# A four-layer graph attention network on one core: transposed blocks of the load stage in two PSUM banks, two segments a round

## The reference

```python
def layer(x, adj, W, a, slope):
    Wh = x @ W
    e = (Wh @ a[:64, 0])[:, None] + (Wh @ a[64:, 0])[None, :]
    e = jnp.where(e > 0, e, slope * e)
    attention = softmax(jnp.where(adj > 0, e, NEG), axis=1)
    return elu(attention @ Wh)
x = layernorm(x + layer(x, adj, W0, a0, 0.2))     # and three more
```

## Time and profile before

| | |
|---|---|
| runs | 601.85 us median (600.64 to 601.86) |
| span of the profiled execution | 859.9 us; the page gives no other time of it |
| granted clock of TensorE, mean | 0.815 |
| PE busy | 419.1 us (49%) |
| DVE busy | 349.6 us (41%) |
| ACT busy | 400.8 us (47%) |
| POOL busy | 278.0 us (32%), 292 gathers of 951 ns |
| ACT masks (L839) | 31 of 3.70 us, the last at 277.3 us |

### The profile page before, as it was taken

One profiled execution on the slowest core, in us unless ns is written; L12 is line 12 of the kernel. 1 busy time (PEld: TensorE's weight loads), 2 busy tenths in 40 slices (PEclk: granted clock), 3 DMA queues, 4 the chain that ended last, 5 costly groups with the idle time before them and its releaser, 6 DMA issues.

```text
span 859.9 us, 10681 instructions
## 1 busy us (share of the span) xinstructions
PE 419.1 (49%) x3453; PEld 334.5 (39%) x3453; DVE 349.6 (41%) x1601; ACT 400.8 (47%) x876; POOL 278.0 (32%) x296
## 2 busy tenths in 40 slices
PE   2354512246655786411129983310499633104985
PEld 1243301245543675300119862210397522004964
DVE  3035813744379598200003872300048622000587
ACT  2677612555476476200325971231269612313684
POOL 0000173140320410777710034777100437771000
PEclk9999999999999998555559995755599857555997
DMA  8999962482673100222200012222000112220000
GB/s 312 428 330 428 422 198 58 173 290 100 212 282 124 17 26 27 32 27 27 27 8 2 20 30 29 28 27 27 9 1 20 34 26 27 28 28 6 8 19 28
DMA packets 20546, 84.86 MB, mean 99 GB/s; under 512 B 6083, under 2 KB 11462, under 8 KB 16262
## 3 DMA queue, kind: packets, MB, share of 16 engines
q1 hardware_dynamic: 10102, 73.15, 21.8%
q0 software_dynamic: 9344, 9.89, 9.4%
q10 hardware_dynamic: 1040, 1.08, 0.4%
HBM read 78.72 MB, written 5.37 MB: 98 GB/s over the span
## 4 chain that ended last, share of the span: by engine, by line
another core or an unknown queue 23%; PE 17%; DVE 12%; ACT 11%; issue 9%; DVEq 0%; ACTq 0%
PE bank L709 7%; ACT arena L865 4%; PE bank L689 3%; PE bank L672 3%; ACT arena L851 2%; DVE x L1313 2%; PE bank L670 1%; DVE stats L1295 1%; PE bank L705 1%; ACT arena L875 1%; DVE arena L1232 1%; ACT arena L839 1%; PE bank L574 1%; DVE res L1292 1%
## 5 line engine op out<-in xcount | busy, mean ns | idle before, releaser
L528 POOL DMA_INDIRECT xg<-table,index x292 | 277.8, 951 | 499.4 <-DMA table<-wh 299.8
L1232 DVE CUSTOM_DVE_ANT_0 arena<-bank,arena 128x256 f32<-128x256 f32 (+3 forms) x123 | 63.4, 523 | 284.7 <-ACT arena L851 224.5
L851 ACT ACTIVATE arena<-bank,sloped_own 128x256 f32<-128x256 f32 (+3 forms) x123 | 68.5, 557 | 176.3 <-remote 109.7
L689 PE MATMUL bank<-packed,arena 128*128 128x128 f32 x339 | 68.3, 323 | 120.0 <-issue 74.0
L839 ACT ACTIVATE arena<-arena,half 128x4096 bf16<-128x4096 int32 x31 | 114.7, 3703 | 19.1 <-DMA arena<-in_adj_t 18.5
L689 PEld LDWEIGHTS bank<-packed,arena 128*128 128x128 f32 x339 | 46.0, 165 | 132.7 <-issue 118.5
L875 ACT COPY arena<-bank 128x256 f32<-128x256 f32 (+3 forms) x123 | 54.1, 446 | 75.4 <-remote 55.4
L670 PE MATMUL bank<-off_row,wall 128*128 128x256 bf16 (+3 forms) x132 | 43.9, 332 | 81.2 <-issue 58.4
L709 PE MATMUL bank<-xg,arena 128*128 128x64 f32 x486 | 73.0, 284 | 10.6 <-ACT arena L875 8.6
L709 PEld LDWEIGHTS bank<-xg,arena 128*128 128x128 f32 x486 | 63.7, 197 | 24.0 <-ACT arena L875 13.5
L1029 DVE MAX8 top<-bank 128x8 f32<-128x256 f32 x31 | 13.4, 431 | 131.5 <-remote 69.5
(11 more groups left out here) (148 smaller groups left out, 780.1 us busy)
## 6 DMA issues: line engine op xcount, KB each, us to landing
arena<-in_adj_t SPq DMA_DIRECT2D x31, 2048.0 KB
xg<-table,index POOLq DMA_INDIRECT x292
table<-wh SPq DMA_DIRECT2D x24, 132.0 KB, 1.7
arena<-in_adj SPq DMA_DIRECT2D x1, 2048.0 KB, 12.9
table<-wh ACTq DMA_DIRECT2D x1, 1056.0 KB
x<-in_x SPq DMA_DIRECT2D x1, 1024.0 KB, 15.0
out_x<-x SPq DMA_DIRECT2D x8, 128.0 KB, 1.9
packed<-in_c_packed SPq DMA_DIRECT2D x1, 312.0 KB
```

Source lines behind the costliest of these rows:

```text
L528: pool.indirect_dma_start(out=xg[:, c, :], out_offset=None, in_=table[l][0:rows, :], in_offset=bass.IndirectOffsetOnAxis(ap=index[:, c:c + ...
L689: t = nc.tensor.transpose(turned_ps[turned_bank(n)][:, c * P:(c + 1) * P], scores(l, n)[:, c * P:(c + 1) * P], ident[:, :])
L851: nc.scalar.activation(scores(l, n)[:, 0:m * P], score_ps[n % len(score_ps)][:, 0:m * P], ACT.Relu, bias=sloped_own[:, k:k + 1], scale=ALP ...
L1232: nc.vector.tensor_tensor_reduce(out=y, in0=score_ps[n % len(score_ps)][:, 0:m * P], in1=y, scale=-1.0, scalar=-FLOOR, op0=ALU.add, op1=AL ...
```

## The change

`KNOWN_MAX` goes from 3 to 2. Segments below `LATE` alternate between bank 5 and bank 7. Bank 7 is free between the last use by the load stage's projections and the first projection for layer 1, and two waits guard these ends: segment 1, the first in bank 7, waits until DVE has read the sum of layer 0 out of it, and layer 1's first projection waits until the last segment of the load stage in bank 7 (segment 19) has been copied.

```diff
-KNOWN_MAX = 3
+KNOWN_MAX = 2
...
 def turned_bank(n):
-    return n % 2 if n >= LATE else 0
+    return 0 if n % 2 == 0 else 1 if n >= LATE else 2
...
+LOAD_TURNED = max(n for n in range(LATE) if turned_bank(n) == 2) + 1
...
-        turned_ps = [banks[5], banks[0]]
+        turned_ps = [banks[5], banks[0], banks[7]]
...
                 pe.wait_ge(xt_copied, n + 1)
+                if n == GROUPS:
+                    pe.wait_ge(turned_copied, LOAD_TURNED)
...
                     pe.wait_ge(xt_copied, GROUPS)
+                if n == 1:
+                    pe.wait_ge(sum_copied, 1)
```

## The result

The changed kernel takes **576.68 us** (median of 4 runs, 575.02 to 578.31) against 601.25 us for the kernel before on the same chip (4 runs, 600.33 to 601.86): ratio 0.9599, 95% interval 0.957 to 0.9627. It is faster by 24.6 us, where 21.6 were forecast.

What follows compares the result with a forecast made beforehand. Bound: a chain of waits, PE and ACT taking turns over one bank. Terms -21.2 (turns), -1.4 (ahead of mask 19), +1.0 (behind mask 23) sum to -21.6 us: 601.85 to 580 us, forecast range 576 to 584 (0.61).

Steps and rivals of the forecast that it cites:

- The span: Whole profile: 859.9 us against 601.85 us timed; timed runs lack its standstills, so savings carry over in microseconds.
- The turns: Load stage, masks 19 to 23: PE and ACT alternate over one bank; 49.26 us becomes 27.15, counted as -21.2.
- a late PE: Masks 19 to 23: about 0.9 us of the old 49.26 is PE issuing late, left out of the saving.
- The round with the lists: PE's third two-segment round, pack of mask 21, also does list matmuls: 7.78 us instead of 7.15.
- Ahead of mask 19: ACT before mask 19 has two fewer exponentials, 2 x 0.71 us: -1.4 us.
- Behind mask 23: Group 5's combine moves behind DVE's list step of batch 5: +1 us taken, bounds 0 and +5.3.
- the 0 that I chose between 0 and 2: Masks 28 to 30, segments of tiles 1 and 2: possible further gain of 0 to 2 us, taken as 0.
- Half comes back: Rival: DVE's 5.3 us list step exposed at beats 20 and 24 loses 10.6 us again: 591 us; chance 0.15.
- No change: Rival: timed load stage is paced by something the profile distorts, such as gathers: 601.85 us; chance 0.13.
- slower: Rival: turns off the timed path, combine behind the list step at beat 25 costs up to 5.3: 607 us; chance 0.06.
- More: Rival: all 23.7 us of ACT's waits for PE go, plus 1.4 and 2 us: 575 us; chance 0.05.

Runs made afterwards that it cites:

- the second profile: The kernel before, unchanged, timed and profiled once more: 601.44 us, ratio 0.9998.
- b: The changed kernel with KNOWN_MAX back at 3, so two banks but up to three segments a round: 591.93 us, ratio 0.9841.
- g: The changed kernel with the pack of block rows 22 to 30 issued twice on PE, same result: 584.08 us, ratio 0.9732.
- d: The kernel before with PE's spread moved to the front of its round in all of layer 0: 603.36 us, ratio 1.0042.

## Why the prediction was right

**The span.** The inference that timed runs do not stand still as in the earlier trace rows held: the second profile spans 597.7 us, and the saving carried over in microseconds. A run is longer than its span from the first to the last instruction by 577.08 - 575.2 = 1.9 us here. The Trainium skill ("Runtime: NRT & Kernel Launch", section "The ~15µs preamble/postamble breakdown") has the profile's total some 6.2 us longer than the timed run; no run here gives that total, so the constant can be neither borne out nor refused, and the prediction's comparison with the span of 859.9 us was not a test of it either.

**The turns.** Mask 19 to mask 23: 27.15 us were worked out, 26.09 measured, 48.33 - 26.09 = 22.24 us less. The forecast took 21.2, since it left out 0.9 us for a late PE. Of the four beats (6.51, 6.51, 6.35 and 7.78 forecast; 6.32, 6.43, 6.67 and 6.67 measured) the fourth differs most. The round with the lists was to take 7.78 us and took 6.67: its lists took 0.64 us as forecast, but its 16 aggregates 2.60 us instead of 3.34, and its spread 0.42 instead of 0.78, to be read between 157.09 and 160.11 above. These two make up the whole 1.1 us. From about there on PE's matmuls took less time, and the trace's first entry of the clock, at 158.9 us, is the upper level. The prediction had read the 1.00 of the earlier trace rows as the upper level throughout; its costs come from rows as long as those at 0.50 (the spread of 0.42 us in the earlier trace rows). It had no term for a rise, and the first three beats came out right because PE was no faster in them than before.
The Trainium skill ("TensorE: Matmul & The Clock Gate", section "HAM oscillation — how this bites in real kernels") reports of another kernel that a second PSUM buffer "gave no further gain". That does not carry over to this one: the bank alone is worth 9 us (b), with two segments a round 24.6.

**Ahead of mask 19.** From mask 16 to mask 19 it took 24.72 us instead of 26.32: 1.6 us, 1.4 forecast.

**Behind mask 23.** The forecast took +1 for the combine behind the list step, in bounds of 0 and 5.3; it was 0. The changed kernel's DVE, and then its ACT:

```profile
173.22 1.39 DVE L1057 MAX8 nbr<-cand 128x8 f32<-128x256 f32 x4
...
178.46 0.42 DVE L1239 CUSTOM_DVE_ANT_0 score<-bank,score 128x256 f32<-128x256 f32 x1
...
178.81 0.42 DVE L1258 TENSOR_TENSOR lone<-sum_wh,lonely 128x256 f32<-128x256 f32 x1
```

```profile
178.92 0.51 ACT L872 ACTIVATE score<-score,seg_max 128x256 f32<-128x256 f32 x1 [2.06 <-DVE seg_max L1239]
...
180.56 0.42 ACT L887 ACTIVATE elow<-num 128x256 f32<-128x256 f32 x1 [1.04 <-DVE num L1273]
```

The list step takes 5.24 us, as in the earlier trace rows, and ACT waits behind it for 2.06 and 1.04 us. But the beat ahead, which has lost the combine, is shorter: distances 5.47, 4.97, 8.88 and 5.08 us instead of 5.66, 5.82, 8.70 and 4.22, the same sum. It was a swap altogether. Masks 27 to 30, where tiles 1 and 2 follow, take 21.29 us and took 21.18: the 0 that I chose between 0 and 2.

**What the prediction did not have.** The tail is 2.3 us longer, 2.0 of it in the stretch that goes with the lower clock. The forecast had nothing there. Layers 1 to 3 are 1.0 us shorter (306.4 against 307.4 us), for which I have no cause. In the sum to the first gather of layer 1: mask 30 comes 23.84 us earlier, the gather 290.30 - 268.77 = 21.5 us, the end of the span 22.5 us. The medians are 24.6 us apart; the 2 us between are less than the 3.3 us over which the runs of the changed kernel scatter. That the forecast of 21.6 us came so near to the 22.5 us of the spans is in part luck: 3.3 us that it did not have were gained (1.0 in the turns, 0.3 ahead of them, 1.0 at the combine, 1.0 in layers 1 to 3) and 2.4 us that it did not have were lost (2.3 in the tail, 0.1 at masks 27 to 30).

**The rivals.** Half comes back: no; ACT's waits for DVE's list step are the 3.1 us above, and the beat before pays for them. No change, and slower: no. More: its 23.7 us of waits came nearly whole (22.24 in the four beats), its 2 us at tiles 1 and 2 did not. The median of 576.68 us lies nearer to this rival's 575 us than to the sum's 580 us.

## What to carry to other kernels

Where two engines hand a buffer to and fro, count how many hand-overs of one round fall behind the reader's *next* long instruction. Here the second buffer paid in full only once the round had no more hand-overs than buffers, and either edit alone could look as if the buffer were not the matter (9 and 1 us, together 24.6). An engine's idle time is cover for extra work only if it lies behind that work on the path; idle time ahead of it, spent on the input, hides nothing (g: 1.35 us each time, 7.4 us in all). An order that helps one stage is to be read through in every stage that shares the code (d lost 9.4 us in the tail). And a printed clock of 1.00 is to be set against the duration of one and the same matmul before anything is built on it (g).

## What the hardware showed unexpectedly

By the changed kernel's view the granted clock fell from 1.00 to the lower level (1.2 GHz) at 165.7 us, directly behind the stretch in which PE was busiest:

```profile
135.50:165.60 30.10, 27.16 (x275) 24.60 (x274) 22.02 (x82) 28.77 (x36) 15.84 (x17) 1.00 0.97 355
165.60:175.80 10.20, 8.95 (x97) 8.11 (x97) 8.21 (x36) 10.20 (x14) 3.82 (x4) 0.51 1.00 304
```

The duration of one matmul, the first of a spread (128x256, bf16), shows that it had not been at the upper level before 158.9 us. In the changed kernel this matmul took 0.42 us at 145.56 and 0.27 us at 159.69 (both shown above), and behind the fall 0.42 us again; the next matmul followed after 0.21, 0.10 and 0.21 us. The row behind the fall; then two rows of before, in the load and in the tail; then one of g, in the load:

```profile
168.92 0.42 PE L675 MATMUL bank<-off_row,wall 128*128 128x256 bf16 x1
```

```profile
205.11 0.42 PE L670 MATMUL bank<-off_row,wall 128*128 128x256 bf16 x1
...
260.13 0.27 PE L670 MATMUL bank<-off_row,wall 128*128 128x256 bf16 x1
```

```profile
169.16 0.42 PE L676 MATMUL bank<-off_row,wall 128*128 128x256 bf16 x1
```

In the changed kernel all 75 of these matmuls that stand inside an entry of 1.00 (the upper level, 2.4 GHz) took 0.27 us, and all four inside an entry of 0.50 took 0.42 us; in before it is 74 and one. Where there is no entry and the views print 1.00, none was that short in any of these kernels. So the changed kernel did not lose a clock that before had. Its matmuls, unlike those of before, sped up inside the stretch from mask 19 to mask 30: for some 7 us from 158.9 us on, after PE had worked without a gap from 139.23 us, and again for shorter times. They slowed again at 165.7 us, after PE had waited 1.43 us for a mask (to 165.32 us). In g, with PE busy 25.70 of 27.20 us between masks 19 and 23, they did not speed up before 215 us. What makes the clock rise or fall stays open. Only one execution of each kernel was profiled in detail, and the others differ: the mean granted clock, in which time without an entry counts as 1.00, runs from 0.867 to 0.925 over the changed kernel's four runs and from 0.856 to 0.930 over g's five. The price that can be read off, with entries on both sides, is that of the tail, some 2 us.
